# A transformer of three layers: another route and an earlier turn for the first head groups of queries and keys

## What is computed

```
x = L0(x, cond)                       # rotation of x in a 64-wide subspace: QR of P, expm of a skew matrix
def layer(x, cond):                   # L1, L2, L3 share this form
    sh1, sc1, g1, sh2, sc2, g2 = split(silu(cond) @ w_ada + b_ada, 6)
    h = layernorm(x) * (1 + sc1) + sh1
    q, k, v = split_heads(h @ w_qkv + b_qkv)        # 16 heads of 18
    # L2 only: q, k = layernorm over the 18 of each head, times gain, plus bias
    o = softmax(q @ k.T / sqrt(18)) @ v
    x = x + g1 * (o @ w_proj + b_proj)
    h = layernorm(x) * (1 + sc2) + sh2
    # L1, L2: dense MLP 288 -> 1152 -> 288 with gelu
    # L3: gate to 4 experts, each token takes its best 2, softmax of the two gates
    return x + g2 * mlp(h)
```

## Time and profile before

| | |
|---|---|
| three runs | 1821.71, 1823.70, 1829.12 us |
| the profiled execution, its own time | 1822.59 us |
| its span | 1820.8 us |
| TensorE (PE) busy | 1643.5 us, 90% |
| weight loads (PEld) | 1068.6 us, 59% |
| VectorE | 1227.4 us, 67% |
| ScalarE | 1055.5 us, 58% |
| GpSimd | 674.1 us, 37% |
| transfers from stage to heads_t, L907 | 120, each 252 KB wide at most |
| transfers from heads_t to QK, L924 and L926 | 384 |

### The profile page before, as it was taken

How to read it: one execution, slowest core, us unless ns; L and a number is a source line. 1 busy time by engine, 2 the same in 40 slices (tenths; PEclk the granted TensorE clock), 3 DMA queues, 4 the chain that set the end, 5 groups by cost and what they waited for, 6 DMA issues and landing times.

```text
span 1820.8 us, 28323 instructions
## 1 busy us (share of the span) xinstructions
PE 1643.5 (90%) x9431; PEld 1068.6 (59%) x9431; DVE 1227.4 (67%) x2685; ACT 1055.5 (58%) x1897; POOL 674.1 (37%) x661
## 2 busy tenths in 40 slices
PE   5876899998899897999899999999988989999997
PEld 2433444443488663444336976444435878999997
DVE  7872677775265576767733656777763776888885
ACT  2322476756546346776674533767667556777773
POOL 4431222213356332433244533223233373343442
PEclk9996799998899888999989999999999999999999
DMA  7721333223000222232310021333322445566662
GB/s 245 245 92 43 94 109 106 90 89 89 28 4 1 81 68 90 70 98 68 118 50 21 1 92 50 103 107 90 95 87 73 123 137 165 162 169 174 171 172 46
DMA packets 106768, 178.16 MB, mean 98 GB/s; under 512 B 14331, under 2 KB 61107, under 8 KB 106335
## 3 DMA queue, kind: packets, MB, share of 16 engines
q1 hardware_dynamic: 100336, 167.07, 30.1%
q0 software_dynamic: 6288, 9.29, 2.7%
HBM read 124.73 MB, written 51.09 MB: 97 GB/s over the span
## 4 chain that ended last, share of the span: by engine, by line
PE 62%; DVE 11%; ACT 9%; DMA 6%; issue 5%; POOL 3%; SPq 3%; ACTq 0%; DVEq 0%; POOLq 0%
PE ps L2184 21%; PE ps L2269 12%; PE ps L2237 8%; PE ps L2223 7%; PE ps L2347 6%; PE ps L2205 4%; DMA heads_t<-stage 3%; ACT Pr L2018 3%; PE ps L2323 1%; DMA raw<-in_w 1%; DVE negmax L1412 1%; DVE GT L1338 1%; PE ps L2074 1%; ACT HQ L1993 1%; SPq L924 1%
## 5 line engine op out<-in xcount | busy, mean ns | idle before, releaser
L1412 DVE TENSOR_REDUCE negmax<-ps 128x1 f32<-128x512 f32 x768 | 488.1, 680 | 219.7 <-PE ps L2205 215.8
L2018 ACT ACTIVATE Pr<-ps 128x512 f32<-128x512 f32 x768 | 410.9, 602 | 212.1 <-PE ps L2223 211.9
L2223 PE MATMUL ps<-QK 55*128 55x512 f32 x768 | 238.4, 512 | 37.3 <-ACT Pr L2018 25.8
L2269 PE MATMUL ps<-W2a,G 128*128 128x288 f32 x1512 | 230.7, 300 | 9.6 <-DVE G L1775 5.7
L2269 PEld LDWEIGHTS ps<-W2a,G 128*128 128x128 f32 x1512 | 213.8, 190 | 21.4 <-DVE G L1775 13.1
L2237 PE MATMUL ps<-Pr,V 128*32 128x512 f32 x1536 | 220.4, 648 | 0.0
L2205 PE MATMUL ps<-QK 54*128 54x512 f32 x768 | 194.8, 439 | 21.2 <-DMA QK<-HQ 7.8
L2223 PEld LDWEIGHTS ps<-QK 55*128 55x128 f32 x768 | 91.9, 190 | 201.1 <-ACT Pr L2018 107.9
L2184 PE MATMUL ps<-HQ,W1a 128*128 128x512 f32 (+3 forms) x756 | 182.0, 381 | 7.3 <-ACT g L2034 5.9
L1775 DVE TENSOR_TENSOR G<-g,G 128x512 fp32r<-128x512 f32 (+1 forms) x201 | 152.4, 763 | 40.7 <-ACT G L2045 36.4
L1169 POOL TENSOR_TENSOR HQ<-act,HQ 128x512 fp32r<-128x512 f32 (+3 forms) x72 | 93.0, 1292 | 190.2 <-ACT HQ L1993 134.2
(11 more groups left out here) (294 smaller groups left out, 2670.2 us busy)
## 6 DMA issues: line engine op xcount, KB each, us to landing
QK<-heads_t SPq DMA_DIRECT2D x192, 144.0 KB
heads_t<-stage SPq DMA_DIRECT2D x96, 252.0 KB
raw<-in_w SPq DMA_DIRECT2D x34, 576.0 KB
raw<-in_w SPq DMA_DIRECT2D x38, 432.0 KB
QK<-heads_t SPq DMA_DIRECT2D x192, 72.0 KB
tok_rows<-blank SPq DMA_DIRECT2D x4, 2700.0 KB, 20.8
XG<-tok_rows SPq DMA_DIRECT2D x11, 540.0 KB, 4.8
WP<-in_w SPq DMA_DIRECT2D x39, 144.0 KB, 3.5
```

The lines of the kernel that those rows point to most:

```text
L1412: dve.tensor_reduce(negmax[:, m % 2, h, t:t + 1], ps[:, row_bank(l, s, i), :], AX, ALU.max, negate=True).then_inc(a_free, 1)
L2018: act.activation(Pr[:, t % 2, 2 * half + pair, :], ps[:, (16 * s + u) % 3, :], ACT.Exp, scale=SCALE).then_inc(b_free, 1)
L2223: mm(ps[:, k % 3, :], QK[r:r + QROW + 1, g, 1, pair, 128 * t:128 * t + 128], QK[r:r + QROW + 1, g, 0, pair, :], start=True, stop=True).the ...
L2269: ins = mm(ps[:, t, 0:C], g_at(n)[:, x, 128 * t:128 * t + 128], W2[w_ % 2][:, w, ft, :], start=ft == 0 and p == 0, stop=ft == FT - 1 and p ...
```

## The change

Four parts.

1. *The opening.* For batch 0 of layer 0 the heads 0 to 7 (group 0) of pieces 0 and 1 go from `stage` straight to their places in `QK`, one transfer for each head and part (`place_first`: 21 for piece 0, 3 for piece 1, each 18 x 512 of four bytes). The eight placing transfers of that group are dropped. Pieces 0 and 1 are still spilled, for the other group, but piece 0 behind piece 1. ScalarE waits for all 24 direct transfers too before it writes pieces 2 and 3 (in `stage`).
2. *Layer 1's tables.* Pieces 0 and 1 are transposed earlier in the attention windows (ticks 6, 7 for 7, 9), one tile of V later (11 for 6), the placing of group 0 earlier (9 for 11). At the passage from layer 0 the two pieces and the placing go one and two ticks forward, and the first scores one tick back.
3. *GpSimd's lag of `root`* is 2 instead of 3, which moves the multiply of QN.
4. *The wait for the banks.* The first three key scores of layers 1 and 2 wait for one bank each instead of the first one waiting for all four.

```
@@ module level
+FIRST = 16 * 16
@@ attention_window, l == 1
-            out += [(t, "place", l, y, g) for g, t in enumerate((11, 16, 24, 32))]
+            out += [(t, "place", l, y, g) for g, t in enumerate((9, 16, 24, 32))]
...
-            out += [(t, "qk", l, y, j) for j, t in enumerate((7, 9, 14, 17, 27))]
-            out += [(t, "v", l, y, k) for k, t in enumerate((4, 6, 15, 22))]
+            out += [(t, "qk", l, y, j) for j, t in enumerate((6, 7, 14, 17, 27))]
+            out += [(t, "v", l, y, k) for k, t in enumerate((4, 11, 15, 22))]
@@ dense_window, v == 2, n == 1
-            out += [(16, "qk", n, 0, 0), (17, "qk", n, 0, 1)]
-            out += [(t, "place", n, 0, g) for g, t in enumerate((20, 25))]
+            out += [(15, "qk", n, 0, 0), (16, "qk", n, 0, 1)]
+            out += [(t, "place", n, 0, g) for g, t in enumerate((18, 25))]
@@ dense_window, v == 3, n == 1
-            out += [(3 + w, "warm", n, w, 0) for w in range(16)]
-            out += [(13, "max", n, 0, 0)]
+            out += [(4 + w, "warm", n, w, 0) for w in range(16)]
+            out += [(14, "max", n, 0, 0)]
@@ LAG, "POOL"
-    root=3
+    root=2
@@ SP
+            def place_first(j):
+
+                key = ("qk", 0, 0, j)
+                sp.wait_ge(low_done, HELD[key] + 1)
+                z = QKS[key] % 2
+                for h in range(7 * j, min(7 * j + 7, 8)):
+                    r, row = HALF * (h % 4 // 2), HD * (h - 7 * j)
+                    places = ((0, 0), (HD, 1), (QR2, 0)) if h < 4 else ((0, 0), (QR1, 0), (QR1 + HD, 1))
+                    for first, part in places:
+                        sp.dma_start(QK[r + first:r + first + HD, 0, h // 4, h % 2, :].bitcast(F32),
+                                     stage[row:row + HD, z, part, :].bitcast(F32)).then_inc(qk_in[0], 16)
...
-                        spill(l, i, k)
+                        if (l, i) == (0, 0) and k < 2:
+                            place_first(k)
+                        if (l, i, k) != (0, 0, 0):
+                            spill(l, i, k)
+                        if (l, i, k) == (0, 0, 1):
+                            spill(l, i, 0)
+                    elif (kind, l, i, k) == ("place", 0, 0, 0):
+                        pass
@@ ACT, before a piece is taken out of its bank
+                        if (l, i) == (0, 0) and k in (2, 3):
+                            act.wait_ge(qk_in[0], PLACED + FIRST + 32)
@@ PE, scores for the maxima
-                    pe.wait_ge(qk_in[g], PLACED * (B * l + s // 4 + 1) + 32 * (l + 1))
+                    pe.wait_ge(qk_in[g], PLACED * (B * l + s // 4 + 1) + 32 * (l + 1) + (FIRST if g == 0 else 0))
@@ PE, scores for the exponential
+                elif l > 0:
+
+                    pe.wait_ge(acc_free, TT * (WBASE[l] - 1) + k + 1)
                 elif k == 0:
-                    if l > 0:
-                        pe.wait_ge(acc_free, TT * WBASE[l])
-                    else:
-                        pe.wait_ge(a_free, 16)
+                    pe.wait_ge(a_free, 16)
```

More of the change, by code:

```diff
@@ L362 @@
                 gturn=0, weigh=0, rank=0, table=0, mod=0, split=1, ext=0, gsum=0),
-    "POOL": dict(gexp=0, setup=0, scatter=0, yadd=0, mean1=1, mean2=1, ln1=1, ln2=1, lng=1, qk=1, out=1, proj=1, tok=1, root=3, split=1, centre=1, fin=1, wg=1,
+    "POOL": dict(gexp=0, setup=0, scatter=0, yadd=0, mean1=1, mean2=1, ln1=1, ln2=1, lng=1, qk=1, out=1, proj=1, tok=1, root=2, split=1, centre=1, fin=1, wg=1,
                  ones=0, vones=0),
```

## The result

The changed kernel is slower: 1829.8 us in the median of 16 runs against 1823.8 us of the kernel before in 16, ratio 1.0041 with a 95% interval of [1.0022, 1.0060] (the two medians alone give 1.0033). A second series (`after_again`) gave 1.0060 [1.0030, 1.0091]; one of its 12 runs took 2833.71 us, against 1817 to 1841 us for the others, and is left out as a slow one. The forecast was 1817.5 us, 0.34% faster, with a range of 1808 to 1826 us. The profiled execution of the changed kernel took 1823.8 us, which was the quickest of its 16; its span is 1821.8 us, so the two profiles alone would say "no change". The shares of the chain say no more: TensorE 62% again.

A forecast was written before the change was run, and what follows sets the result against it. TensorE makes 62% of the chain of waits, so savings count only where it idles. Terms +5.0 - 3.8 - 1.4 - 6.0 + 0 + 0 = -6.2 us on 1822.6 us: 1816.4 us, or 1817.5 us beside the median; range 1808 to 1826 us.

The forecast's parts named there:

- The opening: Layer 0's start: 24 direct issues on SP delay piece 0's spill, then ScalarE and TensorE; +5.0 us, bounds +0 and +9.7.
- rival A: Opening: direct issues are cheap, 0.365 us each, so it costs 0; -11.2 us in all, 1812.5 us; chance 0.33.
- Group 0 was not late: Opening: TensorE's first scores did not wait for group 0's placing, so the direct way saves nothing there.
- The passage and the first tick: Passage into layer 1, -3.8 us, and its first attention tick, -1.4 us: shorter TensorE waits.
- The term for GpSimd's passes: Passage into layer 1: POOL's two long passes over X move into TensorE's stall, worth 1.1 us.
- The relaxed wait's 0.5 us: First attention tick of layer 1: key score 0 waits for one row block of rowt, not four; 0.5 us left.
- The first window: First attention window of layer 1: TensorE's 4.8 us wait for group 0 goes, plus 1.2 us low clock; -6.0 us.
- rival B: First window: ScalarE's Exp chain replaces the stall, only 2 of 6.0 us remain; -2.2 us, 1821.5 us; chance 0.13.
- The second and third window: Layer 1's later attention windows: -0.5 us each from earlier pieces, +0.6 us each from QN; together 0, bounds -2.0 and +3.6.
- lost to the same queue later anyway: Second and third window: two thirds of the 1.8 us wait for squares already lost before, leaving +0.6 us each.
- The passage into layer 2: Passage into layer 2: TensorE's next query score waits for a placing transfer despite the relaxed wait; 0, bounds 0 and -0.5 us.
- Rival C: Opening: SP's queue held up at 0.96 us an issue; +2.3 us in all, slower, 1826.0 us; chance 0.09.

The follow-up runs named there:

- after_again: The changed kernel, unchanged, run and profiled once more against the kernel before; ratio 1.0060 [1.0030, 1.0091].
- before: The kernel before the change, in its first profile; 1823.8 us in the median of 16 runs.
- before_again: The kernel before, unchanged, run and profiled once more; ratio 0.9995 [0.9970, 1.0021].
- pass_only: The kernel before with only the new tables at the passage into layer 1, old wait for all four banks kept; ratio 0.9950 [0.9922, 0.9978].
- pass_wait: The kernel before with the new tables at the passage into layer 1 and the relaxed wait for the banks; ratio 0.9972 [0.9943, 1.0001].
- spill_first: The changed kernel with each piece spilled before its direct transfers instead of piece 0 last; ratio to the kernel before 1.0035 [1.0017, 1.0053].

## Why the prediction was wrong, step by step

The means of the stages over all profiles with the old and the new code of that stage give the change's parts: opening +13.0 us (196.0 for 183.0), 255 to 288 -6.6 us (207.9 in 13 profiles for 214.5 in 5), 288 to 336 -5.9 us (59.9 for 65.8), 336 to 448 +7.7 us (145.0 for 137.3), sum +8.2 us. Two series of timings say +7.5 and +10.9 us. The three other columns are left out of this sum. They scatter by up to 9 us with one program (489.5 and 498.9 us from 448 to 767 in the changed kernel), and in the last one 4 to 5 us stay open, as said above, so that the agreement of the sum with the timings is in part luck.

1. *The opening: a failing step, the right mechanism with its term mis-sized (+5.0 forecast, bound +9.7; +10.2 between the two profiles).* It is over the 8 us at which the prediction called itself wrong. The chain SP's issues, spill, ScalarE, TensorE is there link by link, and rival A's cheap issues are not. The price of an issue was 0.745 us for 0.62 us: 17.9 us for 14.9. The spill of piece 0 was issued at 183.90 us for 180.9 us and took 7.45 us, so it landed at 191.35 us, 3 to 4 us behind my 187.1 to 188.4 us. And TensorE, after 14.9 us idle, did piece 3's product in 3.21 us for 1.88 us, a cost of the wait that my sum did not have. A further 2.9 us comes in by the means, because the profiled opening of `before` was a long one of its kind (185.9 us for a mean of 183.0 us). "Group 0 was not late" holds for that profile; in `before_again` TensorE waited 0.68 us for it.
2. *The passage and the first tick: right in sign, -5.2 us forecast, -6.6 us measured.* The wait shrank by 3.9 us, from 7.10 us to 3.24 us, where I had said near 4 us. The term for GpSimd's passes, 1.1 us without a row behind it, stands against a wait of 1.52 us that is gone. The relaxed wait's 0.5 us stands against 0.76 us in the rows of `pass_only` and `pass_wait`, and no gain in the ratios.
3. *The first window: the number right, -6.0 us for -5.9 us, and that by luck.* The wait of 4.82 us for group 0 went, but a wait of 3.26 us for Exp took its place, which is rival B's mechanism, and TensorE's idle time fell by 1 to 2 us (means 9.4 and 8.3 us, the two profiles 11.0 and 9.3 us) and not by 4.8 us. The rest of the gain came with the granted clock, 0.88 for 0.79 in the two profiles, for which I had booked 1.2 us. That the long wait for the transfer is what the low clock followed is likely, with 17 to 24 us at the low clock around it in three other profiles of the old order, but no run here shows it by itself.
4. *The second and third window: the other failing step, 0 forecast with a bound of +3.6 us, +7.7 us measured.* I named the new wait for squares (1 to 2 us; VectorE 1.71, TensorE 1.97) and then called two thirds of it "lost to the same queue later anyway". None of it was: with the lag alone TensorE's idle time is up by 4 us in the two windows, twice the 1.97 us. And I booked the earlier pieces as a gain of 0.5 us a window. They put two evacuations ahead of the table loads, and TensorE's wait for the Exp behind them grew from 0.83 to 3.27 us, with 1.57 us of another wait gone: with the tables alone the idle time is up by 4 us too. In the first window the new wait stood against the 4.8 us stall, here against nothing of that size.
5. *The passage into layer 2: 0 forecast, no difference beyond the scatter of that stage.* TensorE's wait for the row of ones there is 1.25 and 1.47 us in the changed kernel's profiles for 0.72 and 0.69 us before: as forecast, the transfer sets the time.

Steps 1 and 4 together are 8.0 + 7.7 us, and steps 2 and 3 take 1.3 us off: 14.4 us between the forecast sum of -6.2 us and the +8.2 us of the stages. Rival C had the right place and the right sign (SP held up by its own queue), at too high a price for an issue (0.96 us for 0.745 us). By its own terms it decides from 0.87 us an issue; that the kernel came out slower took the windows' loss as well.

## What to carry to other kernels

Moving transfers off a slow route helps only where the engine stands waiting for them; here the wait was nothing in one profile and 0.68 us in another, and 24 small issues on one queue held up the two that another engine waited for. An edit that removes a stall in one window may bring a wait elsewhere, and the same edit in the windows without that stall leaves only the wait: apply it where the stall is. Before a sum is made against one profile, ask which of its stages would come out the same in a second one, and set idle time and granted clock beside each stage's length: a stage can come out as forecast by the wrong one of the two.

## What the runs showed of the hardware

- An issue from SBUF to SBUF of 18 rows of 2 KB cost SP 0.697 us (0.745 us from one to the next), more than twice the 0.326 us of 18 rows from DRAM. The second such issue behind a spill took 1.59 and 1.68 us (`spill_first`). From the end of the last issue to the release of the waiting engine were 1.9 us there; a spill issued behind the direct transfers released it 7.45 us after its first issue.
- With one program the stages of two executions differ by up to 9 us each (489.5 and 498.9 us at a granted clock of 0.98 and 0.96), where TensorE's granted clock falls at other places: 4.37 us or 2.33 us for the same 14 matmuls.
- After 14.93 us idle TensorE did seven matmuls of 128x512 in 3.21 us for 1.88 us, at a granted clock of 0.52 from 182 to 196 us.
- VectorE's cast into G (128x512) took 2.12 us beside a GpSimd pass over 128x1152, 1.09 us beside one over 126x512, and 0.41 us with GpSimd idle. Its tensor-tensor operation on G took 1.65 us beside a pass over 126x512, and 0.69 us where that pass was over.
